# First expert on all 2048 tokens of two batches while the first search runs, in place of its pass over 512 gathered tokens

## The reference

```python
x = x + 0.5 * ffn(layernorm(x))      # x: 4 batches x 1024 tokens x 128
x = x + attn(layernorm(x))
x = x + 0.5 * ffn(layernorm(x))

def ffn(x, gate_w, w_gate, w_up, w_down):          # 8 experts, inner width 512
    k = S // E * 2                                  # 256 tokens per expert and batch
    affinity = softmax(einsum('bsd,ed->bse', x, gate_w)).transpose(0, 2, 1)
    gating, idx = top_k(affinity, k)
    x_in = x[bidx, idx]
    h = silu(einsum('bekd,eid->beki', x_in, w_gate)) * einsum('bekd,eid->beki', x_in, w_up)
    x_e = einsum('beki,edi->bekd', h, w_down)
    return zeros_like(x).at[bidx, idx].add(gating[..., None] * x_e)
```

## Time and profile before

| | |
|---|---|
| median of 3 runs | 1197.24 us (1195.34 to 1200.41) |
| the profiled execution | 1198.01 us, its span 1196.2 us |
| busy in the span | PE 1079.0 us (90%), DVE 909.9 (76%), ACT 777.1 (65%), POOL 614.0 (51%) |
| PE busy from 20 to 40 us, from 40 to 60 us | 4.17 us, 2.91 us |
| passes of the first layer | from 68.68 us to the end of the last down matmuls at about 283.8 us |

### The profile page before, as it was taken

How to read it: one execution, slowest core, us unless ns; L and a number is a source line. 1 busy time by engine, 2 the same in 40 slices (tenths; PEclk the granted TensorE clock), 3 DMA queues, 4 the chain that set the end, 5 groups by cost and what they waited for, 6 DMA issues and landing times.

```text
span 1196.2 us, 23692 instructions
## 1 busy us (share of the span) xinstructions
PE 1079.0 (90%) x8860; PEld 468.3 (39%) x8860; DVE 909.9 (76%) x1491; ACT 777.1 (65%) x1471; POOL 614.0 (51%) x626
## 2 busy tenths in 40 slices
PE   6189999898699999999999999999998889999993
PEld 6066666664232222222222222222222255666752
...
GB/s 279 30 52 126 93 112 138 91 120 220 105 85 82 94 44 28 36 63 43 54 32 22 63 43 76 27 24 63 77 45 22 28 79 121 85 92 102 113 103 30
DMA packets 93066, 93.97 MB, mean 79 GB/s; under 512 B 14684, under 2 KB 70108, under 8 KB 92920
## 3 DMA queue, kind: packets, MB, share of 16 engines
...
...
## 4 chain that ended last, share of the span: by engine, by line
PE 43%; DVE 18%; issue 15%; ACT 13%; POOL 6%; SPq 2%; DMA 2%; another core or an unknown queue 0%; DVEq 0%; POOLq 0%; ACTq 0%
DVE mx L1919 12%; ACT Pt L1177 11%; PE pO L1506 7%; PE pA L1366 6%; PE pS L1354 6%; PE pS L1527 4%; PE pA L1442 3%; PE pO L1355 3%; PE pS L1355 3%; POOL out_dram L662 3%; DVE ge L1602 2%; PE pA L1334 2%; POOL xg L639 2%; PE pS L1270 2%; ACT U L1168 1%
## 5 line engine op out<-in xcount | busy, mean ns | idle before, releaser
L1919 DVE TENSOR_REDUCE mx<-pA 128x2 f32<-128x1024 f32 x512 | 585.3, 1214 | 16.4 <-PE pA L1442 15.5
L1177 ACT ACTIVATE Pt<-pS 128x512 f32<-128x512 f32 x1024 | 556.3, 596 | 31.6 <-PE pS L1527 23.2
L1506 PE MATMUL pO<-Pt,Vst 128*16 128x256 f32 x4096 | 322.2, 387 | 12.5 <-ACT U L1168 12.5
L639 POOL DMA_INDIRECT xg<-zd,idx x128 | 128.2, 1001 | 145.5 <-DVE idx L1726 74.3
L1067 ACT ACTIVATE Pt<-pS 128x512 f32<-128x512 f32 x128 | 76.3, 596 | 194.6 <-PE pS L1354 160.9
L1442 PE MATMUL pA<-Kst,Qst 48*128 48x512 bf16 x704 | 137.8, 389 | 17.6 <-DVE mx L1919 14.3
L1506 PEld LDWEIGHTS pO<-Pt,Vst 128*16 128x16 f32 x4096 | 68.1, 94 | 204.9 <-issue 108.3
L1527 PE MATMUL pS<-Qst,Kst 51*128 51x512 bf16 x704 | 138.2, 389 | 5.9 <-ACT Pt L1177 2.1
L729 POOL TENSOR_TENSOR mparts<-mx,onesm 128x32 bf16<-128x32 f32 x16 | 4.0, 252 | 268.3 <-DVE mx L1924 212.0
L1354 PE MATMUL pS<-Pt,wg 128*128 128x512 f32 x256 | 138.4, 623 | 2.7 <-issue 1.4
L1366 PEld LDWEIGHTS pA<-wd,Pt 128*128 128x128 f32 x960 | 113.1, 192 | 15.6 <-issue 15.5
...
## 6 DMA issues: line engine op xcount, KB each, us to landing
...
```

The source lines that it names most:

```text
L639: pool.indirect_dma_start(xg[p][:, k, :], None, zd[j // E % 2], bass.IndirectOffsetOnAxis(idx[j % 6][:, k:k + 1], 0)).then_inc(s_gath[p], 16)
L1177: S.activation(Pt[:, s % 4, j, r * 512:(r + 1) * 512], pS[:, bank_of(k, 4 * s + 2 * j + r), :], ACT.Exp, scale=SCALE).then_inc(s_exp, 1)
L1506: last = M.matmul(pO[32 * h:32 * h + 16, cols], Vst[k][:, s % 8, h, :], Pt[:, s % 4, h // 2, (h % 2) * 512 + 256 * a:(h % 2) * 512 + 256 * ...
L1919: V.reduce_max(mx2[:, k, 2 * j:2 * j + 2, c, half], pA[ring[q, a] % 2][:, :, :], AX.X).then_inc(s_Ar, 1)
```

## The change

Expert 0 of batches 0 and 1 no longer gets a list. PE applies its gate, up and down weights to all 2048 tokens straight from ZT: 16 steps (`whole_step`, four blocks of 512 tokens by four chunks of the inner width) and four blocks of down matmuls (`whole_down`). ACT takes the silus (`whole_silu`) and copies the results out (`whole_rows`), DVE makes the products (`whole_product`). The steps are put among the rounds of the search on PE, ACT and DVE; the last blocks stand behind the search. `whole_gains` makes a gain for each token, which is zero where the expert didn't choose it, and `whole_sum(b)` adds gain times result to X in SBUF in pass 1; SP writes that as the start of x1 for batches 0 and 1, in place of the copy of x in DRAM. Pass 0, with one-hots, list, gather, transposes and scatter, is left out, and so are ten warming matmuls. The affinities of half 0 lie in another buffer (scr), since ZT is still read. On POOL `by_slot` stands ahead of the first gathers. The front of the second half begins one place later and its logits move from (1, 4) to (2, 0). The deviations of batches 2 and 3 stand on ACT behind the last silu and ahead of `whole_rows(2)`; in pass 1 `normalise` fills the first three places.

```diff
     place = {}
-    for n in range(NF):
-        place[divmod(4 + n, 4)] = ("f", 1, n)
-    place[1, 4] = ("g", 1)
+    for n, at in enumerate([(1, 1), (1, 2), (1, 3), (1, 4), (2, 1), (2, 2), (2, 3), (2, 4)] +
+                           [divmod(4 + n, 4) for n in range(8, NF)]):
+        place[at] = ("f", 1, n)
+    place[2, 0] = ("g", 1)
     place[8, 0] = ("s", 0)
     place[11, 0], place[11, 1], place[11, 3], place[11, 4] = [("s", m) for m in range(1, 5)]
     for m in range(5, 15):
...
+        first_affT = scr[:, 0, :]
+        first_aff = scr[:, 1, :].rearrange("p (c j r) -> p c j r", c=CH, j=8)
+        whole_y = scr[:, 2:4, :].rearrange("p i (k d) -> p (i k) d", d=D)
+        whole_gain = sb("whole_gain", [P, CH, HB], F32)
...
+        whole_hid = [[hid[0][:, i, :] for i in range(IC)], [hid[1][:, i, :] for i in range(IC)],
+                     [U[i // 2][:, i % 2 * 512:(i % 2 + 1) * 512] for i in range(IC)], [hid[0][:, i, :] for i in range(IC)]]
...
             for a, b in ((turn[:, :], t["turn"]), (wqT[:, :, :], t["wqkT"]), (wq[:, :, :], t["wqk"]), (bq[:, :], t["bqk"]),
                          (wv[:, :], t["wv"]), (wo[:, :], t["wo"]), (bvc[:, :], t["bv"]),
                          (bo[:, :], t["bo"].partition_broadcast(P)), (cos[:, :], t["cos"]), (sin[:, :], t["sin"])):
                 sp.dma_start(a, b).then_inc(s_aconst, 16)
+            load_weights(2)
             store_z(2)
             store_z(3)
+            for b in range(HB):
+                sp.wait_ge(s_sum, b + 1)
+                for i in range(2):
+                    sp.dma_start(x1_in[b][:, 4 * i:4 * i + 4, :], X[:, b * CH + 4 * i:b * CH + 4 * i + 4, :]).then_inc(s_init[b], 16)
             def store_parts(u):
                 b, op = u // 2, u % 2
...
                 pool.wait_ge(s_upper, hh + 1)
+                pool.wait_ge(s_vals, 6 * hh + 6)
                 GP.tensor_tensor(to[:, :, :, 1, :], v, high, ALU.mult).then_inc(s_rest_above, 1)
...
             gains(0)
-            gather(0)
+            by_slot(0)
             gather(1)
-            by_slot(0)
+            gather(2)
             pool.wait_ge(s_aconst, 16 * 10)
             GP.tensor_tensor(bvb[:, :], ones[:, :], bvc[:, 0:1].to_broadcast([P, D]), ALU.mult).then_inc(s_bvb, 1)
-            for it in range(RUN):
+            for it in range(1, RUN):
                 if it + 2 < RUN:
                     gather(it + 2)
-                if it:
+                if it > 1:
                     scatter(it - 1)
                 if it == 2:
...
                     setup(key[1])
-                if (it, k) == (0, 1):
-                    deviation(2)
-                    deviation(3)
-                if (it, k) == (0, 3):
-                    normalise(2, 0, 4)
-                if (it, k) == (0, 4):
+                if (it, k) == (1, 0):
                     normalise(2, 4)
-                if (it, k) == (1, 0):
+                if (it, k) == (1, 1):
                     normalise(3, 0, 4)
-                if (it, k) == (1, 1):
+                if (it, k) == (1, 2):
                     normalise(3, 4)
                 if (it, k) == (10, 3):
                     deviation(4)
...
             normalise(1, 4)
-            for n in range(2, 8):
+            def whole_silu(n):
+                act.wait_ge(*step_done(s_whole_gate, s_gate, n))
+                if n >= 2:
+                    act.wait_ge(*step_done(s_whole_hid, s_hid, n - 2))
+                S.activation(sg[:, n % 2, :], pG[n % 2], ACT.Silu).then_inc(*step_signal(s_whole_silu, s_silu, n))
+            def whole_rows(t):
+                act.wait_ge(*block_done(s_whole_down, s_down, t))
+                S.activation(whole_y[:, 4 * t:4 * t + 4, :].rearrange("p k d -> p (k d)"), pY, ACT.Copy
+                             ).then_inc(*block_signal(s_whole_y, s_ye, t))
+            for n in range(2, 5):
                 front(0, n)
-            act.wait_ge(s_lexp, 1)
-            S.activation(warm[:, :], sd[:, 0:8], ACT.Silu)
-            turn_tokens(0)
-            for it in range(RUN):
+            for n in range(2):
+                whole_silu(n)
+            for n in range(5, 7):
+                front(0, n)
+            for n in range(2, 13):
+                whole_silu(n)
+            for t in range(2):
+                whole_rows(t)
+            for n in range(13, 16):
+                whole_silu(n)
+            deviation(2)
+            deviation(3)
+            whole_rows(2)
+            normalise(2, 0, 4)
+            whole_rows(3)
+            act.nop().then_inc(s_xt, 1)
+            turn_tokens(1)
+            for it in range(1, RUN):
                 expert(it)
...
                 M.matmul(bank_of_use(("f", 0, 4))[:, k * E:(k + 1) * E], ZT[:, k * P:(k + 1) * P], gate_t[:, 0:E], start=True, stop=True)
-            for n in range(2, 8):
+            def whole_step(n):
+                t, i = divmod(n, IC)
+                if n == 0:
+                    pe.wait_ge(*was_read(("f", 0, 3)))
+                    pe.wait_ge(s_w[0], 32)
+                if n >= 2:
+                    pe.wait_ge(*step_done(s_whole_hid, s_hid, n - 2))
+                M.matmul(pG[n % 2], wg[0][:, i * P:(i + 1) * P], ZT[:, t * 512:(t + 1) * 512], start=True, stop=True
+                         ).then_inc(*step_signal(s_whole_gate, s_gate, n))
+                M.matmul(pU[n % 2], wu[0][:, i * P:(i + 1) * P], ZT[:, t * 512:(t + 1) * 512], start=True, stop=True
+                         ).then_inc(*step_signal(s_whole_up, s_up, n))
+            def whole_down(t, first, end):
+                if first == 0:
+                    pe.wait_ge(*step_done(s_whole_hid, s_hid, 4 * t + 3))
+                    if t == 0:
+                        pe.wait_ge(s_wd[0], 16)
+                        pe.wait_ge(*was_read(("f", 0, 4)))
+                    else:
+                        pe.wait_ge(*block_done(s_whole_y, s_ye, t - 1))
+                for m in range(first, end):
+                    k, i = divmod(m, IC)
+                    last = M.matmul(pY[:, k * D:(k + 1) * D], whole_hid[t][i][:, k * P:(k + 1) * P], wd[0][:, i, :],
+                                    start=(i == 0), stop=(i == IC - 1))
+                if end == 16:
+                    last.then_inc(*block_signal(s_whole_down, s_down, t))
+            for n in range(2, 5):
                 front(0, n)
+            for n in range(2):
+                whole_step(n)
+            for n in range(5, 8):
+                front(0, n)
+            whole_step(2)
             pe.wait_ge(s_const, 16 * 8)
-            for n in range(8, NF):
-                front(0, n)
-            compact(0)
+            for r in range(ROUNDS):
+                front(0, 8 + r)
+                whole_step(3 + r)
+                if r >= 2:
+                    whole_down(0, 2 * (r - 2), 2 * (r - 1))
+            front(0, 8 + ROUNDS)
+            whole_down(1, 0, 6)
+            front(0, 9 + ROUNDS)
+            whole_down(1, 6, 12)
+            front(0, 10 + ROUNDS)
+            whole_down(1, 12, 16)
+            whole_step(13)
+            pe.nop().then_inc(s_comp, 1)
             compact(1)
-            warm_up(10)
-            turn_tokens(0)
-            for it in range(RUN):
+            whole_step(14)
+            compact(2)
+            whole_step(15)
+            whole_down(2, 0, 16)
+            whole_down(3, 0, 16)
+            pe.nop().then_inc(s_xtr, 1)
+            turn_tokens(1)
+            for it in range(1, RUN):
                 expert(it)
...
                     use(key)
-                if (it, k) == (0, 2):
-                    scale_and_shift(2)
-                    scale_and_shift(3)
+                if (it, k) == (1, 2):
+                    whole_sum(0)
+                if (it, k) == (1, 4):
+                    whole_sum(1)
                 if (it, k) == (6, 0):
                     all_onehots(8)
...
             dve.wait_ge(s_fill, 3)
-            for n in range(NF):
+            def whole_product(n):
+                dve.wait_ge(*step_done(s_whole_silu, s_silu, n))
+                dve.wait_ge(*step_done(s_whole_up, s_up, n))
+                if n >= 12:
+                    dve.wait_ge(s_whole_down, 1)
+                V.tensor_tensor(whole_hid[n // IC][n % IC], sg[:, n % 2, :], pU[n % 2], ALU.mult
+                                ).then_inc(*step_signal(s_whole_hid, s_hid, n))
+            def whole_gains():
+                V.scalar_tensor_tensor(whole_gain[:, :, :], slotT[:, :, 0].rearrange("p (c b) -> p c b", b=HB), 0.0,
+                                       half[:, :, :].rearrange("p c (b e) -> p c b e", b=HB)[:, :, :, 0],
+                                       ALU.is_ge, ALU.mult).then_inc(s_whole_gain, 1)
+            def whole_sum(b):
+                dve.wait_ge(s_whole_gain, 1)
+                dve.wait_ge(*block_done(s_whole_y, s_ye, 2 * b + 1))
+                for c in range(CH):
```

(30 more changed lines are left out.)

73 lines of the change are left out of this document (43 added, 30 removed).

## The result

| | before | after |
|---|---|---|
| median | 1198.03 us (1195.34 to 1200.81, 20 runs) | 1201.60 us (1198.52 to 1204.74, 20 runs) |
| ratio, 95% interval | | 1.0031 [1.0022, 1.0040] |
| profiled execution | 1198.01 us, span 1196.2 | 1201.23 us, span 1199.3 |

What follows compares the result with a forecast made beforehand. PE was taken to bound the passes but to wait in the first search; +5.4 - 3.57 + 0.2 + 0.5 = +2.5 us gave 1199.7 us beside 1197.24. Range 1195 to 1205; for 8 in 10, 1192 to 1207.

Steps and rivals of the forecast that it cites:

- Start of the search: Two whole steps ahead of the first scan and a third before the first round delay the first `step` by 2.6 us.
- The rounds: In the first search, the product on DVE makes rounds 2.65 us instead of 2.35; +2.7 us, ends 0 and +5.5.
- Rival A: In the search the clock doesn't stay up; at 0.50 a round takes 4.5 us, total 1218 us; chance 0.12.
- Rival C: Fourth block not held, product in DVE's idle time, steps ahead of search at full speed; 1187.7 us; chance 0.06.
- To the first list: From the last round to the first list: waits for down and `by_slot` contention; indices 7.0 us later in all.
- the term for `by_slot`: Beside DVE's one-hots ahead of the first list, POOL slows DVE by 0.5 us, ends 0 and 2.1.
- step 4: From the first list to pass 1: moments hold the fourth down block, clock falls; pass 1 at 85.0, +5.4 us.
- Passes 1 and 2: Pass 1 loses down, -3.57 us; ACT wait +0.2; `whole_sum` costs nothing; front and affinities +0.5 (0 to 1.5).
- the moved logits: Logits moved to (2, 0) leave pass 1 and lengthen pass 2; the sum is zero.
- Rival B: Behind the list, the fourth block isn't held by the moments and follows the third at once; 1193.4 us; chance 0.13.
- Rival D: A wait for weights or the x1 write puts the steps behind the search again; some 20 us; chance 0.03.

Runs made afterwards that it cites:

- cut product: Changed kernel with products 3 to 12 on DVE writing 8 of 512 columns; 1199.14 us, ratio 1.0003 to the kernel before.
- the pause filled: Changed kernel with `whole_rows(2)` ahead of the deviations, plus 6 matmuls of constants on PE ahead of `compact(1)`; 1196.51 us, ratio 0.9998.
- before's second execution: The kernel before, unchanged, run and traced once more; 1196.01 us, ratio 0.9991.
- the copy edit: Changed kernel with `whole_rows(2)` ahead of the two deviations on ACT, nothing else; 1195.64 us, ratio 0.9976.
- the whole steps behind the search: Changed kernel with `whole_rows(2)` ahead of the deviations and all 16 steps and 4 down blocks behind search and lists; 1228.53 us, ratio 1.0245.
- both pauses gone: Changed kernel with `whole_rows(2)` ahead of the deviations and `by_slot` waiting for expert 1's one-hots; 1192.47 us, ratio 0.9947.

## Why the prediction was right

The forecast was 1199.7 us, the median 1201.60; the mechanism came as forecast, with its parts at these sizes.

1. **Start of the search.** First scan at 28.19 (forecast 28.65), first `step` at 31.29 (31.65): +2.2 us against +2.6. The first whole step ran at half clock and the second partly, as taken. That rise was taken from pass 0, where it came 5 us after the work began; here PE had worked nearly without a pause since 10.77 us, at half clock from 12 us on, so that the two agree is luck.
2. **The rounds.** 2.617 us (2.65), clock 1.00 throughout, bound by DVE; +2.4 against +2.7. The cut product puts the price at 0.33 a round (0.30). The range of the sum had left out this step's own ends (0 and +5.5); the measured +2.4 didn't need them. Rival A is out: there was no half clock in the search, nor a swing as the Trainium skill (TensorE: Matmul & The Clock Gate, section A second HAM failure mode: psum-queue depth-cycling) describes it for short pauses. Rival C is out too, since it wanted rounds of 2.4 us.
3. **To the first list.** `need` at 57.61 (58.1) and DVE idle for 1.16 us until the first block of down, as forecast. Indices ready 7.6 us later than before (7.0): the term for `by_slot` was mis-sized, 1.4 us where 0.5 was taken. The Trainium skill's rule (SBUF — State Buffer, section Who interferes with whom) had put it near 2.1; the measured 1.4 is nearer to that than to the value taken. POOL's instructions had begun before DVE's, so their two full lengths, as 2.1 has it, were never to be waited for. (The terms named add up to 7.1, not 7.0.)
4. **Behind the list.** Here the forecast fell short: pass 1 at 86.88 instead of 85.0, +7.3 where +5.4 was forecast. The wait ahead of the fourth block (4.24 us, forecast 4.6), its releaser and the block's length (5.29, forecast 5.3) are right. What step 4 didn't see is the half clock ahead of it. It followed the 1.35 us pause before `compact(1)`, which the contention made: from that `compact`'s next step to the second list passed 69.33 - 65.93 = 3.40 us, and 67.93 - 66.13 = 1.80 with the pause filled. The moments ended at 79.11 instead of 76.4. Of these 2.7 us 0.8 came back by luck: from the end of the fourth block to pass 1 the sum had 2.3 us, and 86.88 - 85.36 = 1.5 us passed.
5. **Passes 1 and 2.** Pass 1 is 4.39 us shorter (4.3). `whole_sum` takes 2.19 us twice (2.3) and cost nothing that is seen. That the moved logits sum to zero was right only in the kernel before: pass 2 grew by 1.6 us, of which 0.8 remained at pass 7. The forecast had +0.5 (0 to 1.5) for the front's side work beside it, so what remained lies in its range.

The sum was +2.5; the shift is +3.4 at the list of pass 3, +4.2 at that of pass 7, +5.8 behind pass 11 (the clock), and +3.1 at the end of the span. The attention gives nothing back: the first list of the second layer comes at 951.97 instead of 946.26, +5.7. From it to the sixth list pass 70.05 us instead of 72.45 (71.71 in before's second execution). The granted clock says where: between 970 and 978 us it was 0.67 and 0.90 in four-microsecond windows of before, and between 1006 and 1014 us 0.86 and 0.71, and it was 1.00 in both stretches after; in before's second execution only the later fall is there. So falls of the clock behind pass 7, which the sum doesn't have, move the end of the span by as much as its own terms do, and that the forecast came within 1.1 us of the measured +3.6 is in part luck. Rival B (the fourth block not held) was out in this kernel, but its price was about right: the copy edit brings it about, and took 6.0 us off the median (6.6 by the ratios) where B took 6.3 off the forecast. Rival D is out by the rounds; its price, some 20 us for steps behind the search, came as 24.4 us of delay against the changed kernel.

Where did the gain go? The new work on PE is 41.6 us (16 x 1.71 + 4 x 3.57). Of it 13 steps and two blocks, 29.4 us, stand ahead of the end of the search; three steps and two blocks, 12.3 us, stand behind it and delay pass 1. Laid behind the search as well, they cost as much, 29.4 us (the whole steps behind the search, against the copy alone). That is a balance: the search gets shorter there and other waits come in. But it says that the place beside the search hides most of that work. The pass left out gives back less than what the rest costs: a later search, contention, and the two pauses with the half clock behind each. With both pauses gone the change is a gain, 0.9947.
